# Order of gathers, subtractions and scatters on GpSimd's queue in the expert chunks of a vision-tower kernel

## Chip, cores and metric

The kernel runs on one core of a Trainium2 chip. The metric is the device time of one execution in microseconds (us), as the median of several runs; lower is better.

## What is computed

Thirty-two images of 256 x 256 pass through a wavelet mixing, get a class row in front (257 rows of 256), pass through attention, and then through a mixture of eight experts. Only the last part matters here. Each expert chooses the k rows that score highest for it and adds its result to them:

```python
xf = x.reshape(-1, d)                       # 32 * 257 = 8224 rows, d = 256
k = int(bs * CAPACITY) // n                 # 1028 rows for each of n = 8 experts
vals, idx = jax.lax.top_k(scores.T, k)
kept_w = vals.T
flat_idx = idx.T.reshape(-1)
y = _layernorm(xf[flat_idx].reshape(k, n, d), ln_gamma, ln_beta)
h = jnp.einsum('knd,nfd->knf', y, fc1s) + b1s        # 256 -> 1024
h = jax.nn.gelu(h, approximate=True)
o = jnp.einsum('knf,ndf->knd', h, fc2s) + b2s        # 1024 -> 256
out = xf.at[flat_idx].add((o * kept_w[:, :, None]).reshape(k * n, d))
```

## The kernel before

The program is written engine by engine: each engine has its own instruction list, executed in order, and semaphores tie the lists together. The stage of the experts begins near 340 us and lasts to the end.

**Chunks.** The 1028 rows of an expert are nine tiles (eight of 128 rows, one of 4), and three tiles make a chunk: chunk 0 has tiles 0 to 2, chunk 1 tiles 3 to 5, chunk 2 tiles 6 to 8 (260 columns in all, the "tail"). Here the experts are numbered 0 to 7 in the order in which they are done. `jobs` (L347) walks over the 24 chunks and calls each engine's `emit(prev, cur, nxt, tiles)`: `cur` is the chunk whose first layer is computed, `prev` the one before, whose second layer is computed beside it, `nxt` the one whose rows are turned. A chunk runs in eight slices `f`, one per 128 of the 1024 hidden units.

**Split operands.** Every matmul operand is kept as a high part and a low part (the rest), and three products are summed. So weights and activations are first copied to the high part (`w1h`, `w2h`, `hh`, `yh`), and then the low part is what is left (`w1l`, `w2l`, `hl`, `yl`).

**In a slice** TensorE does six matmuls of the first layer (`first`, L1022) into one of three banks used in turn; ScalarE applies the GELU (L756) and copies the high part (L759); VectorE subtracts for the low part (L1590). TensorE may start slice f only when the low part of slice f-3 is there. Between, TensorE does second-layer matmuls of `prev` (L1036; L1048 for the tail). In slice 3 it turns `nxt`'s gathered rows (`turn`, L1011), which waits for the chunk's gathers.

**Weights.** Both layers of all experts pass through one buffer, `raw`, in two halves. For each half: SyncE loads it (L436) once GpSimd has finished with the half before (`wlo`); ScalarE copies the high part (`high`, L722) in slices 1 and 3; GpSimd subtracts for the low part (`low`, L536), which waits for ScalarE's copy (`whi`). The next expert's first layer (`w1`) is treated in chunk 0 and its second layer (`w2`) in chunk 2. Weight tiles are double: one set for even experts, one for odd.

**Rows in and out.** GpSimd gathers the rows of a tile from DRAM into `yg` (L555) two chunks ahead (`far`), as soon as their indices (`idx`) exist, and scatters each result tile `ob` into the output with an addition (L577), after ScalarE has written it (`weighed`, L772, semaphore `omul`). There are three `ob` buffers; ScalarE writes one again only when its last scatter has landed. In chunks 0 to 2 ScalarE writes the `ob` of chunk c-1 in slices 3, 5 and 7, but those of a tail all in slice 6 of the next chunk 0. `keep_index` (L566, L567) copies an expert's indices for the scatters, in chunk 1.

**Indices.** VectorE makes the indices of an expert two ahead (`place`, L1553 to L1566: `SM`, `rk`, `jk`, `rowf`, `idx`), four tiles of it in chunk 1 and five in chunk 2; with the last tile it prepares the next expert's comparison in two operations over 1028 columns, `ohu` (L1535) and `oh` (L1538). These stand on VectorE ahead of the low part of chunk 2's last slice.

**GpSimd's order.** It is written by hand in `emit` (L589 to L609) and is the same for all chunks of one kind. In chunks 1 and 2 it alternates scatter, gather (and in chunk 2 a subtraction after the second and the third pair); in chunk 0, where the scatters of the tail come last, it is gather, gather, subtraction, gather, subtraction, and then three scatters.

Of the kernel before, what the change touches and what calls it, by code (L numbers as in the profile page):

```python
# [48 lines left out]
def build_program(nc, x, cls_tok, Wa, ba, Wd1, bd1, Wd2, bd2, Wd3, bd3, R, gate_w, gate_wT, gamma, beta,  # L49
                  fc1T, b1, fc2T, b2, b2T, const, out, debug=None):  # L50
    ctx = ExitStack()
    with ctx:
# [206 lines left out]
        def apart(eng):  # L259


            eng.nop(nofuse=True)
# [72 lines left out]
        def flat(weights, half):  # L335

            return weights[:, :, :].rearrange("p a b -> p (a b)")[:, half * NF:(half + 1) * NF]
# [123 lines left out]
        def _(po):  # L461
# [66 lines left out]
            operators(Step(0, 0))  # L528
            po.wait_ge(s["st_set"], 2)
            steps(po, emit, 2)  # L530

            def low(eh, q, layer, half):

                hi, lo = (w1s, w2s)[layer][eh]
                po.wait_ge(s["whi"], (q * 2 + layer) * 2 + half + 1)
                rest = g.tensor_tensor(flat(lo, half), raw[:, half * NF:(half + 1) * NF], flat(hi, half), ALU.subtract)  # L536
                rest.then_inc(s[f"wlo{half}"], 1)
# [12 lines left out]
            def gather(job, t):  # L550

                eh, m = job.eh, SLOTS[t]
                po.wait_ge(s["ixd"], job.q * 9 + t + 1)
                apart(po)
                g.indirect_dma_start(out=yg[eh][0:m, t, :], out_offset=None, in_=rows,  # L555
                                     in_offset=tok(ap=idx[eh][0:m, t:t + 1], axis=0))\
                    .then_inc(s[f"gat{eh}{t // 3}"], 16)

            def keep_index(job):

                eh = job.eh
                if not isinstance(job.q, int) or job.q > 1:
                    for r in range(3):
                        po.wait_ge(s[f"scat{r}"], (job.q - 1) * 48)
                apart(po)
                g.tensor_copy(sidx[eh][:, 0:8], idx[eh][:, 0:8])  # L566
                g.tensor_copy(sidx[eh][0:SLOTS[8], 8:9], idx[eh][0:SLOTS[8], 8:9]).then_inc(s["idc"], 1)  # L567

            def scatter(job, t):
                m = SLOTS[t]  # L570
                po.wait_ge(s["omul"], job.q * 9 + t + 1)
                if t == 0:
                    po.wait_ge(s["idc"], job.q + 1)
                    for r in range(3):
                        after(po, f"scat{r}", job.q * 48)
                apart(po)
                g.indirect_dma_start(out=out_rows, out_offset=tok(ap=sidx[job.eh][0:m, t:t + 1], axis=0),  # L577
                                     in_=ob[t % 3][0:m, :], in_offset=None, compute_op=ALU.add)\
                    .then_inc(s[f"scat{t % 3}"], 16)
# [9 lines left out]
            def emit(prev, cur, nxt, _tiles):  # L589
                split = nxt and cur.q_next and cur.c != 1  # L590

                far = Job(cur.el, cur.k + 2) if cur and (cur.q_next or cur.c == 0) else None
                if far and isinstance(far.q, int) and far.q == 0:
                    far = None

                tail = prev and prev.c == 2
                for u in range(3):
                    if prev and not tail:
                        scatter(prev, prev.t0 + u)
                    if far:  # L600
                        gather(far, far.t0 + u)
                    if split and u:
                        low(1 - cur.eh, cur.q + 1, cur.c // 2, u - 1)
                for u in range(3):
                    if tail:
                        scatter(prev, prev.t0 + u)
                if cur and cur.c == 1 and cur.q_next:
                    keep_index(Job(cur.el, cur.k + 2))
            jobs(po, emit)  # L609


# [1141 lines left out]
```

## Time and profile before

| | |
|---|---|
| median of 3 runs | 786.63 us (785.98 to 787.31) |
| the profiled execution | 786.62 us |
| its span in the trace | 784.8 us |
| TensorE (PE) busy | 696.7 us, 89% |
| VectorE (DVE) busy | 541.0 us, 69% |
| ScalarE (ACT) busy | 459.9 us, 59% |
| GpSimd (POOL) busy | 473.3 us, 60% |

How to read it: times in the trace count from the span's start. An engine is busy while an instruction executes on it; what it waits for in between is given with the engine, the tile and the line that released it. PEld is TensorE's weight load, which lies beside the matmuls, SP is SyncE. An engine that is idle costs nothing by itself; what counts is whether TensorE, or whatever ends last, waited for it. `Lnnn` is a line of the kernel before.

### The profile page before, as it was taken

To read this page: it belongs to the slowest core of one execution; us is meant where nothing else is said; L and a number is where in the kernel's file an instruction comes from. 1 tells how busy PE (TensorE), PEld (TensorE's weight loads), DVE (VectorE), ACT (ScalarE), POOL (GpSimd) and SP (SyncE) were. 2 spreads that over 40 slices of the span, in tenths; PEclk is the share of its full clock that TensorE was granted. 3 is DMA by queue.
4 is the path that set the end of the run, shared out by engine and by line. 5 is a ranking of instruction groups with operands and counts; after the bars stand their busy time and mean duration, and the time that the engine had idled before them with its cause. 6 is when DMAs were issued, how large, how long until landed. Compare 5 with 4: busy or idle time off the path is not lost.

```text
span 784.8 us, 15827 instructions
## 1 busy us (share of the span) xinstructions
PE 696.7 (89%) x4630; PEld 635.5 (81%) x4630; DVE 541.0 (69%) x1885; ACT 459.9 (59%) x1095; POOL 473.3 (60%) x660
## 2 busy tenths in 40 slices
PE   6987999999999945447999999989999999999994
PEld 3986888888888734336989999989889999899993
DVE  3765798998899778987784766756846757634431
ACT  1003588888888869315556656665566566656551
POOL 0258689888988545142366485584674855846523
PEclk9989999999999975559999999999999999999997
DMA  9900022222222228121134243352342432533222
GB/s 258 307 18 1 4 83 81 80 80 81 80 80 81 81 93 170 54 56 61 30 81 117 42 109 89 50 149 43 75 122 41 108 88 42 146 52 49 35 28 27
DMA packets 63563, 64.14 MB, mean 82 GB/s; under 512 B 14032, under 2 KB 57104, under 8 KB 63376
## 3 DMA queue, kind: packets, MB, share of 16 engines
q1 hardware_dynamic: 50576, 46.33, 19.6%
q0 software_dynamic: 12800, 17.12, 13.5%
q8 instruction: 26, 0.43, 0.2%
q14 instruction: 33, 0.27, 0.1%
q10 hardware_dynamic: 128, 0.00, 0.0%
HBM read 37.90 MB, written 25.53 MB: 81 GB/s over the span
## 4 chain that ended last, share of the span: by engine, by line
PE 36%; DVE 7%; issue 6%; ACT 6%; POOL 5%; DMA 3%; POOLq 0%; ACTq 0%; DVEq 0%; SPq 0%
PE bank L1022 16%; PE bank L1036 15%; ACT bank L746 2%; PE bank L1011 2%; PE bank L1048 2%; POOL out L577 2%; POOL w2l L536 1%; POOL yg L555 1%; DMA raw<-in_fc1T 1%; DMA yg<-rows,idx 1%; DVE yl L1583 1%; ACT bank L756 1%; PE bank L1001 1%; DVE jk L1560 1%; ACT hh L759 1%
## 5 line engine op out<-in xcount | busy, mean ns | idle before, releaser
L577 POOL DMA_INDIRECT out<-ob,sidx x72 | 113.9, 1582 | 160.5 <-ACT ob L772 148.8
L1590 DVE TENSOR_TENSOR hl<-bank,hh 128x384 fp32r<-128x384 f32 (+1 forms) x192 | 97.5, 513 | 139.1 <-ACT hh L759 138.6
L756 ACT ACTIVATE bank<-bank,b1s 128x384 f32<-128x384 f32 (+1 forms) x192 | 99.4, 518 | 138.0 <-PE bank L1022 133.5
L1022 PE MATMUL bank<-yh,w1h 128*128 128x384 f32 (+1 forms) x384 | 132.7, 346 | 8.1 <-DVE hl L1590 4.7
L1022 PE MATMUL bank<-yh,w1l 128*128 128x384 f32 (+1 forms) x384 | 123.8, 322 | 0.0
L1022 PE MATMUL bank<-yl,w1h 128*128 128x384 f32 (+1 forms) x384 | 123.3, 321 | 0.0
L1036 PE MATMUL bank<-w2h,hh 128*128 128x256 f32 x384 | 108.1, 281 | 0.0
L1036 PE MATMUL bank<-w2l,hh 128*128 128x256 f32 x384 | 108.0, 281 | 0.0
L1036 PE MATMUL bank<-w2h,hl 128*128 128x256 f32 x384 | 107.9, 281 | 0.0
L555 POOL DMA_INDIRECT yg<-rows,idx x72 | 72.4, 1006 | 44.2 <-issue 39.1
L759 ACT ACTIVATE hh<-bank 128x384 fp32r<-128x384 f32 (+1 forms) x192 | 87.7, 457 | 6.1
L1022 PEld LDWEIGHTS bank<-yh,w1h 128*128 128x128 f32 x384 | 73.8, 192 | 13.0 <-DVE hl L1590 6.0
L1022 PEld LDWEIGHTS bank<-yl,w1h 128*128 128x128 f32 x384 | 73.6, 192 | 0.0
L1022 PEld LDWEIGHTS bank<-yh,w1l 128*128 128x128 f32 x384 | 73.1, 190 | 0.0
L1036 PEld LDWEIGHTS bank<-w2h,hh 128*128 128x128 f32 x384 | 72.7, 189 | 0.0
L1036 PEld LDWEIGHTS bank<-w2l,hh 128*128 128x128 f32 x384 | 72.7, 189 | 0.0
L1036 PEld LDWEIGHTS bank<-w2h,hl 128*128 128x128 f32 x384 | 72.5, 189 | 0.0
L880 PE MATMUL bank<-ET,Rw 128*128 128x256 f32 x256 | 66.1, 380 | 1.7 <-ACT ET L663 1.7
L948 PE MATMUL bank<-GT,ET 128*128 128x137 f32 (+1 forms) x256 | 52.5, 340 | 0.7 <-ACT GT L690 0.7
L504 POOL TENSOR_TENSOR ST<-A,mhalf 128x6 f32<-128x6 f32 x37 | 50.0, 1352 | 3.1
L880 PEld LDWEIGHTS bank<-ET,Rw 128*128 128x128 f32 x256 | 43.8, 191 | 5.6 <-issue 2.1
L290 POOL TENSOR_TENSOR ARENA<-OB,C 128x512 f32<-128x512 f32 x32 | 40.8, 1275 | 12.2 <-ACT OB L637 12.2
(249 smaller groups left out, 1770.6 us busy)
## 6 DMA issues: line engine op xcount, KB each, us to landing
BIG<-in_x SPq DMA_DIRECT2D x4, 2048.0 KB, 16.3
out<-Bs SPq DMA_DIRECT2D x32, 256.0 KB, 2.2
rows<-Yp SPq DMA_DIRECT2D x32, 256.0 KB, 2.4
raw<-in_fc1T SPq DMA_DIRECT2D x16, 512.0 KB
raw<-in_fc2T SPq DMA_DIRECT2D x16, 512.0 KB
yg<-rows,idx POOLq DMA_INDIRECT x72, 2.8
out<-ob,sidx POOLq DMA_INDIRECT x72, 3.8
gwb<-in_gate_w SPq DMA_DIRECT2D x1, 1024.0 KB, 7.2
```

Source lines behind the costliest of these rows:

```text
L290: return ops.tensor_tensor(OP[m.p].rearrange("p g (r k) -> p g r k", k=CG), blocks.unsqueeze(2).to_broadcast(wide), cst("blocks").rearrang ...
L504: g.tensor_tensor(st[:, 8:14], A6[:, :], mhalf[:, :], ALU.pow).then_inc(s["pow"], 1)
L555: g.indirect_dma_start(out=yg[eh][0:m, t, :], out_offset=None, in_=rows, in_offset=tok(ap=idx[eh][0:m, t:t + 1], axis=0))\
L577: g.indirect_dma_start(out=out_rows, out_offset=tok(ap=sidx[job.eh][0:m, t:t + 1], axis=0), in_=ob[t % 3][0:m, :], in_offset=None, compute ...
L746: last = A.activation(sgn[2 * eh + j], V[:, eh, :], ACT.Sign, bias=tried[:, k:k + 1], scale=-1.0, accum_out=cna[eh][:, j:j + 1])
L756: A.activation(h[:, 0:cur.w], h[:, 0:cur.w], ACT.Gelu_apprx_tanh, bias=b1s[:, bass.ds(cur.e, 1), f]).then_inc(s["hact"], 1)
L759: A.activation(hT[cur.p][0][:, f, 0:cur.w], h[:, 0:cur.w], ACT.Copy).then_inc(s["hhi"], 1)
L880: last = T.matmul(Rb[:, e * D:(e + 1) * D], Rw[:, j, e * P:(e + 1) * P], ET[c.p][:, j, 1:NT], start=(j == 0), stop=(j == 1))
L948: T.matmul(Sb[:, c0:c0 + w], ET[c.p][:, j, 1 + h * P:1 + (h + 1) * P], GT[c.p][:, j, 0:w], start=(j == 0), stop=False)
L1022: last = T.matmul(Lb[ring(cur, f)][:, 0:cur.w], w1s[cur.eh][i][:, d, f * P:(f + 1) * P], yT[cur.p][k][:, d, 0:cur.w], start=(n == 0), stop ...
L1036: mm = T.matmul(bank[4 + t % 2][:, 0:D], hT[prev.p][i][:, f, at:at + P], w2s[prev.eh][k][:, f, :], start=(n == 0), stop=(n == 23))
L1590: v.tensor_tensor(hT[cur.p][1][:, f, 0:cur.w], Lb[ring(cur, f)][:, 0:cur.w], hT[cur.p][0][:, f, 0:cur.w], ALU.subtract).then_inc(s["hlo"], 1)
```

## The change

On GpSimd, in each chunk, the three gathers of the far chunk are issued first. Then, for u = 0, 1, 2, the subtraction of half u (in chunks 0 and 2, for u < 2), followed by the scatter u of the previous chunk. The scatters of a tail stay where they were, last in chunk 0. The gather and the scatter themselves, their semaphores and all other engines are as before. Lines from 597 on move by one.

```diff
                 tail = prev and prev.c == 2
+                if far:
+                    for u in range(3):
+                        gather(far, far.t0 + u)
                 for u in range(3):
+                    if split and u < 2:
+                        low(1 - cur.eh, cur.q + 1, cur.c // 2, u)
                     if prev and not tail:
                         scatter(prev, prev.t0 + u)
-                    if far:
-                        gather(far, far.t0 + u)
-                    if split and u:
-                        low(1 - cur.eh, cur.q + 1, cur.c // 2, u - 1)
                 for u in range(3):
                     if tail:
                         scatter(prev, prev.t0 + u)
```

GpSimd's list in chunk 2 of expert 0 (L577 is a scatter of `ob`, L555 a gather into `yg`, L536 a subtraction; the last digit of a name is its buffer), before:

```order
L577 DMA out_0<-ob0,sidx0 8224x256
L555 DMA yg1<-rows,idx1 128x264
L577 DMA out_0<-ob1,sidx0 8224x256
L555 DMA yg1<-rows,idx1 128x264
L536 TENSOR_TENSOR w2l1<-raw,w2h1 128x1024
L577 DMA out_0<-ob2,sidx0 8224x256
L555 DMA yg1<-rows,idx1 128x264
L536 TENSOR_TENSOR w2l1<-raw,w2h1 128x1024
```

and in the change:

```order
L555 DMA yg1<-rows,idx1 128x264 x3
L536 TENSOR_TENSOR w2l1<-raw,w2h1 128x1024
L577 DMA out_0<-ob0,sidx0 8224x256
L536 TENSOR_TENSOR w2l1<-raw,w2h1 128x1024
L577 DMA out_0<-ob1,sidx0 8224x256
L577 DMA out_0<-ob2,sidx0 8224x256
```

The three gathers have moved to the head, the first subtraction from behind the second scatter to ahead of the first, and the second from behind the third scatter to behind the first.

The next place on GpSimd is chunk 0 of expert 1, with the tail's scatters at its end, before:

```order
L555 DMA yg1<-rows,idx1 128x264 x2
L536 TENSOR_TENSOR w1l0<-raw,w1h0 128x1024
L555 DMA yg1<-rows,idx1 4x264
L536 TENSOR_TENSOR w1l0<-raw,w1h0 128x1024
L577 DMA out_0<-ob0,sidx0 8224x256
```

and in the change:

```order
L555 DMA yg1<-rows,idx1 128x264 x2
L555 DMA yg1<-rows,idx1 4x264
L536 TENSOR_TENSOR w1l0<-raw,w1h0 128x1024 x2
L577 DMA out_0<-ob0,sidx0 8224x256
```

Here only the third gather and the first subtraction have changed places.

## Rows read from the trace of the kernel before

**Rows 1.** Page: busy time of each engine.

```profile
PE 696.7 (89%) x4630; PEld 635.5 (81%) x4630; DVE 541.0 (69%) x1885; ACT 459.9 (59%) x1095; POOL 473.3 (60%) x660
```

**Rows 2.** By stretch: length, busy us (count) of PE, PEld, DVE, ACT, POOL, clock, DMA.

```profile
526.96:545.55 18.59, 18.59 (x130) 18.09 (x131) 10.88 (x35) 9.98 (x22) 8.94 (x7) 1.00 0.33 64
545.55:561.82 16.27, 15.87 (x132) 15.38 (x132) 12.31 (x45) 10.66 (x23) 8.19 (x9) 1.00 0.31 51
...
717.76:734.07 16.31, 15.81 (x111) 15.24 (x109) 6.84 (x15) 9.71 (x21) 12.14 (x9) 1.00 0.29 55
```

**Rows 3.** The same view: chunk 0 of experts 1 to 6.

```profile
404.26:421.80 17.54, 16.10 (x111) 15.20 (x109) 11.18 (x22) 11.49 (x23) 15.79 (x10) 1.00 0.48 137
...
561.82:580.09 18.27, 16.10 (x111) 15.21 (x109) 11.54 (x21) 11.45 (x23) 15.98 (x10) 1.00 0.49 133
...
sum 107.12, PE 96.83 PEld 91.25 DVE 68.39 ACT 69.03 POOL 95.69; mean PE 16.14 PEld 15.21 DVE 11.40 ACT 11.51 POOL 15.95
```

**Rows 4.** Line L722 from 340 us: its engine's idle time (us, times), by releaser.

```profile
  DMA raw<-in_fc1T: 24.1, 12
```

**Rows 5.** ScalarE in order of time: start, us, instruction, idle before.

```profile
496.46 1.05 ACT L722 ACTIVATE w2h<-raw 128x1024 fp32r<-128x1024 f32 x1
...
500.63 1.05 ACT L722 ACTIVATE w2h<-raw 128x1024 fp32r<-128x1024 f32 x1
...
515.86 1.06 ACT L722 ACTIVATE w1h<-raw 128x1024 fp32r<-128x1024 f32 x1 [2.44 <-DMA raw<-in_fc1T]
...
521.55 1.06 ACT L722 ACTIVATE w1h<-raw 128x1024 fp32r<-128x1024 f32 x1 [2.51 <-DMA raw<-in_fc1T]
```

**Rows 6.** Chain of waits, in order of time: start, us, what.

```profile
515.17 2.42 POOL w2l L536
...
517.74 3.79 DMA raw<-in_fc1T
...
526.96 1.15 PE bank L1022 x5
```

**Rows 7.** GpSimd in order of time, expert 2's end and expert 3's chunk 0.

```profile
495.21 1.57 POOL L577 DMA_INDIRECT out<-ob,sidx  x1 [1.71 <-ACT ob L772]
...
502.85 1.60 POOL L577 DMA_INDIRECT out<-ob,sidx  x1 [4.42 <-ACT ob L772]
...
506.48 1.57 POOL L577 DMA_INDIRECT out<-ob,sidx  x1 [0.71 <-ACT ob L772]
...
509.40 2.41 POOL L536 TENSOR_TENSOR w2l<-raw,w2h 128x1024 fp32r<-128x1024 f32 x1
511.98 1.85 POOL L577 DMA_INDIRECT out<-ob,sidx  x1 [0.17 <-issue]
...
527.46 1.63 POOL L577 DMA_INDIRECT out<-ob,sidx  x1 [1.55 <-ACT ob L772]
```

**Rows 8.** VectorE in order of time: ohu of expert 0, then around 510.

```profile
350.84 0.73 DVE L1535 TENSOR_SCALAR ohu<-iot,begM 128x1028 bf16<-128x1028 f32 x1
...
509.84 2.54 DVE L1535 TENSOR_SCALAR ohu<-iot,begM 128x1028 bf16<-128x1028 f32 x1
...
513.72 1.35 DVE L1590 TENSOR_TENSOR hl<-bank,hh 128x260 fp32r<-128x260 f32 x3
```

**Rows 9.** TensorE in order of time, at the start of slice 2.

```profile
514.19 0.44 PE L1022 MATMUL bank<-yh,w1h 128*128 128x384 f32 x1 [0.85 <-DVE hl L1590]
```

**Rows 10.** GpSimd in order of time, expert 0.

```profile
350.45 1.25 POOL L555 DMA_INDIRECT yg<-rows,idx  x1 [1.28 <-DVE idx L1566]
...
354.91 2.38 POOL L536 TENSOR_TENSOR w1l<-raw,w1h 128x1024 fp32r<-128x1024 f32 x1 [0.89 <-ACT w1h L722]
```

**Rows 11.** GpSimd in order of time, chunk 1 of expert 3.

```profile
537.89 1.59 POOL L577 DMA_INDIRECT out<-ob,sidx  x1 [5.28 <-ACT ob L772]
```

**Rows 12.** TensorE in order of time, turning rows in expert 7.

```profile
727.44 0.85 PE L1011 MATMUL bank<-C,yg 128*128 128x128 f32 x6 [0.50 <-DMA yg<-rows,idx]
```

**Rows 13.** VectorE in order of time, expert 0.

```profile
356.48 0.27 DVE L1556 TENSOR_SCALAR rk<-C,SM 128x1 f32<-128x1 f32 x1
```

## Prediction

> **What bounds the kernel now.** I read the views from wide to narrow. The page first: TensorE is busy 89% of the span [rows 1], and in the experts' stage its granted clock is full [rows 2, 3], so the stage of the experts, which is all that the diff touches, is bound by TensorE unless something starves it. Then the busy time by stretch, one stretch per chunk, cut where TensorE starts the first matmul of the chunk. Chunk 1 of expert 3 lasts 18.59 us and TensorE is busy for all of it; chunk 2 lasts 16.27 with 15.87 busy [rows 2]. Chunk 0 is another matter: in experts 1 to 6 it lasts 17.54 to 18.27 us, 107.12 in all, with 96.83 busy [rows 3]. Expert 7's chunk 0 has the same matmuls (x111 against x110 or x111) and lasts 16.31 [rows 2]. So there are about 2 us per expert to be had, in chunk 0 and hardly anywhere else.
>
> Who starves it: ScalarE's copy of the next expert's first-layer weights (L722, w1h<-raw) found its engine idle for 24.1 us over 12 times, until the transfer into raw had landed [rows 4]. Twelve is two halves times six experts. The two waits of expert 3 are 2.44 and 2.51 us [rows 5]; everything behind them on ScalarE, the activations of TensorE's products, is late with them. The chain of waits says where this comes from: GpSimd's subtraction w2l (515.17), the transfer into raw (517.74), and then, through ScalarE's copy w1h and the activations behind it, TensorE's next chunk (526.96) [rows 6]. raw is one buffer for both layers, so the first-layer weights are fetched only when GpSimd has subtracted the second-layer ones. GpSimd's own rows show why it subtracts late: both inputs, w2h, were ready in the middle of chunk 2 (copies at 496.46 and 500.63) [rows 5], but the subtractions ran at 509.40 and 515.17 [rows 6, 7], because each stood behind scatters that waited for ScalarE's results (4.42 and 0.71 us idle), and behind gathers queued after those scatters [rows 7].
>
> A second stall stands in the same place. VectorE's ohu takes 0.73 us at 350.84 and 2.54 us at 509.84 [rows 8]. In the second case it ran under GpSimd's subtraction (509.40 to 511.81) and ended 0.57 us after it. VectorE's hl for the last slice of chunk 2 queues behind ohu and oh, starts at 513.72, and TensorE stood 0.85 us for it [rows 8, 9]. So I put the 1.8 us of difference down to GpSimd's subtraction, not to ohu's own work. The Trainium skill (SBUF — State Buffer, SBUF: two separate sides) says that GpSimd and a two-port VectorE operation take a shared port pair as an exclusive lock, the loser blocking fully; by that rule the trace agrees.
>
> **The change, part by part.** No instruction is added or removed; all of it is order on GpSimd.
>
> Chunk 2, the part that matters. GpSimd ends chunk 1's last scatter at 496.78 (495.21 + 1.57) and its index copies 0.3 later. Now come three gathers at 1.0 us and a gap of 0.3 each, until 501.0; their indices were made an expert earlier. The first subtraction needs 2.4 us [rows 7] and w2h's first half, ready at 497.5: it runs 501.0 to 503.4, not 509.40 to 511.81. The first scatter follows (its ob was ready at 502.8, so it is 0.8 late), 1.85 us, then the second subtraction, about 505.6 to 508.1, not 515.17 to 517.59. The two other scatters start near 508.3 (was 506.48) and 510.3 (was 511.98).
>
> - Transfers. ScalarE's copy began 4.05 us after the first subtraction's end (511.81) and 3.96 after the second's (517.59), load and all [rows 5, 6, 7]. With the same lags the halves land at 507.5 and 512.1. ScalarE wants them at 513.42 (515.86 less its 2.44 of waiting) and at 516.6 (521.55 less both waits). Slack 5.9 and 4.5 us: both waits go, even if a transfer took twice as long beside the gathers and scatters.
> - ohu at 509.84 now meets no subtraction, which ended 1.7 us before; a scatter is under way instead. At 350.84 it met a gather (350.45 to 351.70) and took 0.73 [rows 8, 10]. I take 0.73, so VectorE is 1.8 us earlier and TensorE's 0.85 go.
> - The late scatters cost nothing: ob is written again in chunk 0's sixth slice, whose first scatter was at 527.46 [rows 7], over 15 us on.
>
> Chunk 0: gathers, both subtractions, then the tail's scatters. The subtractions wait for w1h, now at about 514.5 and 519, and end near 518.5 and 521.4, ahead of the tail's scatters; their results are wanted an expert later. Costed at nothing.
>
> Chunk 1: three gathers before the first scatter, 4.0 us. The cover is GpSimd's idle 5.28 us there before the scatter at 537.89 [rows 11]. Were it gone, a scatter would be late by the rest, with its buffer free for many us more: still nothing. TensorE is full in chunk 1, so nothing is gained either.
>
> What chunk 0 then lasts: the row nearest is expert 7's, which has no weight copies, no ohu, and the same matmuls: 16.31, of which 0.50 is TensorE waiting for a gather [rows 2, 12]: that of tile 5, which GpSimd's order put behind the last scatter of the chunk before, and which now goes out at that chunk's head. So 15.8. The two copies, 2.1 us of ScalarE, come on top of expert 7's 9.71 busy, 11.8 in 15.8: they fit, and I add nothing for them.
>
> **Sum.** Experts 1 to 6: 6 x 15.8 = 94.8 against 107.12, 12.3 less. Expert 7: 0.5 less. Expert 0: GpSimd's order in chunk 0 is the same, nothing. Together 12.8, so the profiled execution's 786.62 us becomes **773.8**; the median of the runs, 786.63, is the same time. Bounds: below, TensorE's busy time alone in the six chunks gives no more than 107.12 - 96.83 = 10.3, but that busy time includes stretched matmuls (16.1 against 15.8 in expert 7); with 15.6 per chunk and the 0.4 us idle of chunk 2 also gone in seven experts the gain would be 16. Above, half the waits left, see the rivals.
>
> **Rivals.**
> 1. *Only the transfer's waits go.* If gathers take longer and the second subtraction slips by the 1.7 us of margin, it falls on ohu again. TensorE keeps its 0.85 us six times: 773.8 + 5.1 = 778.9. For it: the margin is small and was computed through six GpSimd steps. Against: every step's row repeats within 0.1 us from expert to expert.
> 2. *One of the two transfer waits stays*, or ScalarE, with two copies inside a shorter chunk, becomes the limit of its last four slices. About half of the 2 us per expert comes back: 773.8 + 6 = 780. Against: the slacks of 5.9 and 4.5 us.
> 3. *Slower: the subtractions now hold up VectorE in chunk 2.* There VectorE makes indices (rk, rowf, idx) from SBUF, and TensorE already idles 0.4 us [rows 2]. If each of 14 moved subtractions held one of its operations as long as ohu was held, 1.8 us, that is 25.2 us; less 12.8, the kernel would take 799. It decides from 0.9 us each. Against: rk at 356.48 ran inside a subtraction (354.91 to 357.29) and took 0.27 [rows 10, 13], its usual. The skill's page puts under the lock also operations with two SBUF inputs against a GpSimd that reads SBUF; in chunk 2 only oh is one, and it stands behind ohu.
> 4. *No change.* ScalarE's waits were in the shadow of something else, and chunk 0 keeps its length, 786. Against: expert 7's is shorter by 1.2 us or more.
>
> **How the numbers follow.** Forecast 0.73, rival 1 0.12, rival 2 0.07, rival 3 0.04, rival 4 0.04. The forecast's own range is 771.3 (gain 15.3, chunk 0 near 15.6 and part of chunk 2's idle) to 776.5 (0.5 us per expert less than hoped). The range for 8 in 10 goes on to 779.3, which takes in rival 1 and part of rival 2. A measurement can tell 0.2%, 1.6 us: forecast and rivals 1 and 2 are faster, 0.92; rival 4 is the same, 0.04; rival 3 slower, 0.04.
>
> **What would show it.** Right: no idle time of L722 on raw<-in_fc1T; w2l subtractions that end before ohu begins; all ohu near 0.73 us; chunk 0 near 15.8 us in experts 1 to 6, chunk 1 still 18.6. Wrong: ohu at 2.5 (rival 1); L722 waits of over 0.5 us (rival 2); chunk 2 longer than 16.3 with VectorE named as TensorE's releaser (rival 3); a chunk 0 of 17.5 with some other releaser in ScalarE's place (rival 4).

## Result and the profile after

The changed kernel takes **775.31 us** (median of 4 runs, 774.18 to 777.41) against 786.66 us (785.98 to 787.31) for the kernel before in the same set of runs: a ratio of 0.9859 with a 95% interval of 0.9843 to 0.9874, some 11.3 us less. In a later set of runs it took 773.26 us against 785.69, ratio 0.9847 (0.9833 to 0.986); one execution of the kernel before in that set was slow, 1752.38 us, and stands outside the ratio. The profiled execution of the first set is its longest, 777.41 us, with a span of 775.6.

First the page: GpSimd (POOL) is busy for about as long as before, VectorE (DVE) 10.5 us less [rows 1], since its comparisons are no longer stretched.

```profile
PE 696.2 (90%) x4630; PEld 636.8 (82%) x4630; DVE 530.5 (68%) x1885; ACT 460.9 (59%) x1095; POOL 476.5 (61%) x660
```

Chunk 0 of experts 1 to 6 in the view by stretch (length, then busy us and count of PE, PEld, DVE, ACT, POOL, clock, DMA):

```profile
405.89:421.52 15.63, 15.63 (x111) 15.23 (x109) 9.64 (x22) 11.63 (x23) 9.98 (x6) 1.00 0.45 116
...
506.86:522.65 15.79, 15.64 (x110) 15.24 (x109) 9.77 (x21) 11.69 (x23) 10.72 (x7) 1.00 0.50 122
...
sum 94.52, PE 93.89 PEld 91.48 DVE 58.35 ACT 69.55 POOL 63.20; mean PE 15.65 PEld 15.25 DVE 9.72 ACT 11.59 POOL 10.53
```

94.52 us stand where 107.12 stood [rows 3], and TensorE is busy for 93.89 of them. The same view for chunk 1 and 2 of expert 3 (they answer to [rows 2]), and chunk 0 of expert 7:

```profile
522.65:541.23 18.58, 18.58 (x130) 18.08 (x131) 10.88 (x35) 10.06 (x22) 10.77 (x8) 1.00 0.33 62
541.23:557.71 16.48, 16.10 (x133) 15.45 (x132) 12.12 (x45) 10.56 (x23) 12.20 (x10) 1.00 0.40 83
709.51:725.16 15.65, 15.65 (x111) 15.25 (x109) 6.85 (x15) 9.73 (x21) 6.03 (x5) 1.00 0.23 36
```

Chunk 1 is unchanged. Chunk 2 is 0.21 us longer, and in experts 4 and 5 it is 17.16 and 17.18 us where it was 15.99 and 16.27: the change gave something back there (experiment 5). GpSimd in order of time, around the start of expert 3's chunk 0 at 506.86, where [rows 7] had the subtractions at 509.40 and 515.17 for a chunk that began at 508.70:

```profile
497.54 0.95 POOL L555 DMA_INDIRECT yg<-rows,idx  x1 [0.30 <-issue]
498.52 2.40 POOL L536 TENSOR_TENSOR w2l<-raw,w2h 128x1024 fp32r<-128x1024 f32 x1
501.62 1.62 POOL L577 DMA_INDIRECT out<-ob,sidx  x1 [0.70 <-issue]
502.70 2.98 POOL L536 TENSOR_TENSOR w2l<-raw,w2h 128x1024 fp32r<-128x1024 f32 x1
505.85 1.59 POOL L577 DMA_INDIRECT out<-ob,sidx  x1 [0.17 <-issue]
509.17 2.46 POOL L577 DMA_INDIRECT out<-ob,sidx  x1 [1.72 <-ACT ob L773]
```

The second subtraction now ends at 505.68, before the chunk begins. (Its record overlaps that of the scatter before it, so its start is rough.) VectorE and ScalarE in order of time, for [rows 8] and [rows 5]:

```profile
508.00 0.76 DVE L1536 TENSOR_SCALAR ohu<-iot,begM 128x1028 bf16<-128x1028 f32 x1
508.89 1.29 DVE L1539 SCALAR_TENSOR_TENSOR oh<-iot,finM,ohu 128x1028 bf16<-128x1028 f32 x1
```

```profile
511.48 1.05 ACT L723 ACTIVATE w1h<-raw 128x1024 fp32r<-128x1024 f32 x1
...
515.99 1.05 ACT L723 ACTIVATE w1h<-raw 128x1024 fp32r<-128x1024 f32 x1
```

ohu takes 0.76 instead of 2.54 us, and ScalarE's two weight copies stand without a bracket: no idle time before them. The view of that line (L723 now) has no entry under its idle time, where [rows 4] had 24.1 us:

```profile
its engine sat idle before it (us, times) until:
who waited for it (us, times):
  POOL w1l L536: 2.6, 2
```

### The profile page after: what moved, and what is told of

The parts are those of the page before. It is cut to its first block, busy times and chain, and to the rows that moved or that the text cites. A ratio compares the mean times of both kernels' runs of the same rounds, so it can differ in the third digit from the quotient of the medians.

```text
span 775.6 us, 15827 instructions
## 1 busy us (share of the span) xinstructions
PE 696.2 (90%) x4630; PEld 636.8 (82%) x4630; DVE 530.5 (68%) x1885; ACT 460.9 (59%) x1095; POOL 476.5 (61%) x660
## 4 chain that ended last, share of the span: by engine, by line
PE 44%; DVE 8%; ACT 6%; issue 2%; POOL 1%; another core or an unknown queue 1%; DMA 0%; POOLq 0%; ACTq 0%; DVEq 0%
PE bank L1023 21%; PE bank L1037 14%; PE bank L1049 5%; ACT bank L747 2%; PE bank L1012 2%; DVE yl L1584 2%; DVE jk L1561 1%; ACT bank L757 1%; PE bank L1002 1%; ACT hh L760 1%; ACT jk L747 1%; DVE rk L1557 1%; DVE hl L1591 1%; DVE bank L1576 0%
## 5 line engine op out<-in xcount | busy, mean ns | idle before, releaser
L577 POOL DMA_INDIRECT out<-ob,sidx x72 | 118.1, 1640 | 147.2 <-ACT ob L773 122.5
L555 POOL DMA_INDIRECT yg<-rows,idx x72 | 71.9, 998 | 45.0 <-issue 40.2
```

## Where chunk 0's time went, slice by slice

These sums over experts 1 to 6 are worked out from the starts of TensorE's first matmul of each slice. "The change" is its second profile, where chunk 2 gave back least. The last column is chunk 2 of experts 2 to 5 together.

| kernel | chunk 0 | its slice 1 | slice 6 | slice 7 | chunk 2, experts 2 to 5 |
|---|---|---|---|---|---|
| before | 107.12 | 19.22 | 14.07 | 10.15 | 64.53 |
| the change | 94.45 | 13.51 | 9.69 | 8.42 | 65.42 (first profile 67.24) |
| chunks 0 and 1 alone | 107.10 | 19.10 | 14.46 | 10.13 | 64.55 |
| chunk 2 alone | 94.44 | 13.53 | 9.70 | 8.44 | 64.55 |
| second half last | 97.12 | 13.51 | 11.08 | 9.69 | 65.51 |
| before, ohu not held | 110.02 | 14.11 | 21.24 | 10.35 | 64.71 |
| the change, VectorE later | 102.13 | 20.47 | 9.73 | 8.41 | 64.53 |

Of the 12.7 us, 5.7 come from slice 1 (VectorE behind ohu) and 6.1 from slices 6 and 7 (ScalarE behind the second transfer). The last rows of the table are kernels of the experiments below.

## Experiments

Each kernel was timed against the kernel before on its chip. Line numbers in its rows are its own.

**1. The new order in chunk 2 alone.** NEW and OLD stand for the loops of the diff.

```diff
+                if cur and cur.c == 2:
+                    NEW
+                else:
+                    OLD
```

> GpSimd's new order in chunk 2 alone; in chunks 0 and 1 the order of before. My theory (all of the gain comes from the second-layer subtractions being done 8 to 9 us earlier in chunk 2, which ends ScalarE's waits for raw and the collision with ohu): 775.3 us, within 1.6 us of the change, chunk 0 of experts 1 to 6 near 15.7 us, ohu 0.73 us. Rival (the gathers and subtractions of chunk 0, or the gathers of chunk 1, carry half of it): 780 us or more.

Measured: 773.09 us (771.18 to 773.69), ratio 0.9825 (0.9799 to 0.9852). The whole gain is in chunk 2's order.

**2. The new order in chunks 0 and 1 alone.** The condition is `cur.c != 2`.

> The new order in chunks 0 and 1 alone; in chunk 2 the order of before. My theory: 786.6 us, within 1.6 us of before, ScalarE's waits for raw<-in_fc1T still about 24 us in 12 times, ohu 2.5 us. Rival (half of the gain lies here): 781 us.

Measured: 785.93 us (783.95 to 787.61), ratio 0.9994 (0.9981 to 1.0008): nothing. ohu is held again, and the view of ScalarE's weight copy shows the waits:

```profile
  DMA raw<-in_fc1T: 23.2, 12
```

**3. The change, with VectorE made about 2 us later ahead of ohu.** Three more comparisons into scratch tiles; the transfers stay early.

```diff
+                if not isinstance(job.q, int) or job.q > 1:
+                    for n, spare in enumerate((ge, eq, sc)):
+                        v.tensor_scalar(spare[:, :, :].rearrange("p a b -> p (a b)"), iot[:, 0:2 * NT], 0.0, None,
+                                        ALU.is_ge, ALU.add, accum_out=(need[:, 0:1], need[:, 1:2], mm2[:, 0:1])[n])
```

> The change, with three operations of no use on VectorE (514 columns each, some 2.0 us together) ahead of ohu for the last six experts: the delay that the collision made, without a collision. In the trace of the change the low part hl of chunk 2's last slice is done at 510.6 and TensorE wants it at 511.3. If VectorE's delay has a price of its own, 2.0 us less 0.7 of slack is 1.3 us six times: 783 us. Rival (ScalarE's waits were the whole loss and the 0.85 us of TensorE for hl would have been made up later): 775.3 us, within 1.6 us.

Measured: 781.18 us (780.87 to 783.1), ratio 0.9938 (0.9918 to 0.9958). By the ratios that is 6.2 or 7.2 us more than the change (0.9859 or 0.9847), and in the traces chunk 0 of the six experts is 7.7 us longer. TensorE's waits from 400 to 730 us name VectorE's hl in experts 1 to 6 (engine line, releaser, us, times, longest):

```profile
PE bank L1023 <- DVE hl L1595: 6.0, 6, 1.0
```

Slice 1 is back at 3.35 to 3.46 us (3.01 to 3.28 before, 2.25 in the change), slices 6 and 7 are not. VectorE's hl starts 5.21 us after the start of chunk 0 (513.29 less 508.08), 5.02 in the kernel before and 3.24 in the change, so the delay made here is 0.2 us larger than the one it stands for. A VectorE that is late by 1.8 to 2.0 us then costs TensorE about 1 us per expert, also where no transfer is late: the stretched ohu was a cost by itself, worth about half of the gain.

**4. The kernel before, with an ohu that is not held.** The comparison gets an accumulated output, which makes it another form of instruction.

```diff
-                v.tensor_scalar(ohu[:, c0:c1], iot[:, c0:c1], begM[:, bass.ds(job.el, 1), job.eh], None, ALU.is_ge)\
+                v.tensor_scalar(ohu[:, c0:c1], iot[:, c0:c1], begM[:, bass.ds(job.el, 1), job.eh], None, ALU.is_ge,
+                                ALU.add, accum_out=junk1[:, :])\
                     .then_inc(s[begun], 1)
```

> The kernel before, with ohu written as a comparison that also accumulates its sum (a form that I take not to collide with GpSimd's subtraction, and to last 1.1 to 1.3 us instead of 2.5). GpSimd's order is that of before, so ScalarE still waits for raw. My theory: TensorE's 0.85 us in front of slice 2 goes, but the end of chunk 0 is set by the second transfer's landing, so nothing is gained: 786.6 us, within 1.6 us. Rival (the two stalls add up, each with its own price): 786.6 - 6 x 0.85 = 781.5 us. If ohu still takes 2.5 us, the run says nothing on this.

Measured: 792.46 us (791.3 to 792.98), ratio 1.0079 (1.0056 to 1.0102), **slower** than before, where neither theory had it. VectorE, then GpSimd, in order of time, expert 3:

```profile
511.62 1.28 DVE L1536 TENSOR_SCALAR_CACHE_REDUCE ohu<-iot,begM 128x1028 bf16<-128x1028 f32 x1
512.83 0.08 DVE L1536 DVE_READ_ACCUMULATOR ohu<-iot,begM 128x1 f32 x1
513.04 1.62 DVE L1540 SCALAR_TENSOR_TENSOR oh<-iot,finM,ohu 128x1028 bf16<-128x1028 f32 x1
```

```profile
511.16 2.41 POOL L537 TENSOR_TENSOR w2l<-raw,w2h 128x1024 fp32r<-128x1024 f32 x1
513.74 2.39 POOL L578 DMA_INDIRECT out<-ob,sidx  x1 [0.17 <-issue]
516.43 1.00 POOL L556 DMA_INDIRECT yg<-rows,idx  x1 [0.30 <-issue]
517.46 2.41 POOL L537 TENSOR_TENSOR w2l<-raw,w2h 128x1024 fp32r<-128x1024 f32 x1
```

ohu runs inside the subtraction at 1.28 us, and slice 1 falls by 5.1 us over six experts. oh, which begins 0.53 us before that subtraction ends, takes 1.62 us, not 1.29. And the scatter now starts 0.70 us after oh did, where in the kernel before it started 0.53 us ahead of oh, under the end of ohu; it takes 2.39 us instead of 1.85 [rows 7]. So the second subtraction behind it comes later in the chunk (7.00 us after its start, 6.47 before), and with it the second transfer. ScalarE waits 3.36 us for it, not 2.51 [rows 5], in all 29.6 us over 12 times:

```profile
523.80 1.06 ACT L723 ACTIVATE w1h<-raw 128x1024 fp32r<-128x1024 f32 x1 [3.36 <-DMA raw<-in_fc1T]
```

Slice 6 grows by 7.2 us over six experts. In the kernel before, then, the two delays overlap: taking one away hands its time to the other, with interest. Of the 4.7 us by which the profiled execution (791.30) is longer than that of the kernel before, chunk 0 of these six experts has 2.9; 1.0 lies in expert 0's first two chunks, which differ by as much between the other kernels here, and 0.7 in one chunk 1. Of the kernels run here, those that move the subtractions out of the way are the ones that remove both delays.

**5. The change again.** No edit.

> The changed kernel once more, unaltered. In its first profile ScalarE began the fourth GELU of chunk 2 in experts 2 to 5 1.1 to 1.9 us after TensorE's product was done, and chunk 2 of these experts lasted 16.42 to 17.18 instead of 15.98; the kernel with the new order in chunk 2 alone was 2.2 us faster and showed none of it. Theory 'sporadic': that lateness belongs to the execution; the median stays near 775.3 but this profile shows another pattern, perhaps none, and a profiled execution without it is near 774.7 (777.4 less 2.7). Theory 'order': it belongs to the order of the requests in chunks 0 and 1; then the same four rows are here again, with chunk 2 near 16.4 to 17.2.

Measured: 773.26 us (772.74 to 774.12), ratio 0.9847 (0.9833 to 0.986). The same four rows are late, by 1.02 to 1.06 us now. The first profile, expert 4's chunk 2 in order of time (GpSimd, ScalarE, VectorE; releasers are inferred, so "remote" names no one); TensorE's product was done at 599.16:

```profile
599.21 0.95 POOL L555 DMA_INDIRECT yg<-rows,idx  x1 [0.30 <-issue]
...
600.18 2.41 POOL L536 TENSOR_TENSOR w2l<-raw,w2h 128x1024 fp32r<-128x1024 f32 x1
...
601.01 0.45 ACT L757 ACTIVATE bank<-bank,b1s 128x260 f32<-128x260 f32 x1 [2.89 <-remote]
...
601.91 0.43 DVE L1591 TENSOR_TENSOR hl<-bank,hh 128x260 fp32r<-128x260 f32 x1 [1.76 <-ACT hh L760]
```

The second profile, same place, product done at 596.21:

```profile
596.26 0.96 POOL L555 DMA_INDIRECT yg<-rows,idx  x1 [0.30 <-issue]
...
597.26 0.45 ACT L757 ACTIVATE bank<-bank,b1s 128x260 f32<-128x260 f32 x1 [2.09 <-PE bank L1023]
```

So the place is the kernel's, as the theory 'order' had it, and its size varies: 1.1 to 1.9 us late and 2.7 us more in chunk 2 in the one, 1.0 to 1.1 late and 0.9 more in the other. Usually ScalarE starts 0.10 to 0.12 us after the product. That the orders of chunks 0 and 1 are what matters is not shown by this run.

The lateness reaches TensorE through VectorE: hl, then the layer norm of the turned rows, then the index operation jk queue behind the GELU. TensorE's waits in the first profile, from 400 to 730 us, have (0.3 us, once, in the kernel before):

```profile
PE bank L1002 <- DVE jk L1561: 3.3, 8, 0.8
```

Two things more are in the traces. Experts 2 to 5 are those of the loop in `jobs`; expert 1 is written out ahead of it, has the same gather 0.01 to 0.03 us after the same product in the two profiles, and its GELU is on time (0.10 us). And in neither profile do the DMA queues that load instructions carry a packet from 592 to 606 us, so no loading of instructions is seen at expert 4's late GELU.

**6 and 7. The new order in chunks 0 and 2, and in chunks 1 and 2.** Conditions as in experiment 1, with `cur.c != 1` and `cur.c != 0` for the new order.

> The new order in chunks 0 and 2, the old one in chunk 1. Chunk 0 of experts 1 to 6 stays at 15.6 to 15.9. If the three gathers ahead of the scatters in chunk 1 are what the change loses against the kernel that has the new order in chunk 2 alone (773.1), this one is at 773.1 and chunk 2 lasts 15.98; if chunk 0's order is, it is at 775.3; if neither is and the lateness of ScalarE is sporadic, anything from 773 to 775.3.

> The new order in chunks 1 and 2, the old one in chunk 0 (where it delays the two w1l subtractions until after two gathers). Mirror of the run with chunks 0 and 2: if chunk 0's order is the loss, 773.1; if chunk 1's is, 775.3 with chunk 2 of some experts over 16.4 us. If these two kernels and the change agree within 1 us, neither part is the loss.

Measured: chunks 0 and 2, 776.38 us (774.93 to 776.77), ratio 0.9879 (0.9864 to 0.9895); chunks 1 and 2, 774.08 (772.35 to 774.65), ratio 0.9846 (0.9831 to 0.9861). Neither is simply the loss. The second repeats the change's late GELU (chunk 2 of experts 2 to 5 65.50 us in all). The first loses at another place: in chunk 2 of experts 0 and 2 to 5, VectorE begins the work on the turned rows 1.25 to 1.34 us after TensorE's transposes are done (0.49 in expert 1; 0.03 to 0.04 in the kernel before), and chunk 2 of experts 2 to 5 takes 66.53 us, 2.0 more than in experiment 1; here in expert 4, where they were done at 601.33 (600.51 + 0.82):

```profile
602.63 1.27 DVE L1585 TENSOR_SCALAR bank<-bank,gam,bet 128x384 f32<-128x384 f32 x2 [1.61 <-PE bank L1021]
```

The kernel of experiment 1 has GpSimd's gathers at the same distance from the start of chunk 2 (5.9 us both) and starts that instruction at once (598.97, transposes done 598.93). I had no place for this in either expectation.

**8. The second subtraction behind all three scatters of chunk 2.**

```diff
                 for u in range(3):
-                    if split and u < 2:
+                    if split and (u == 0 or u == 1 and cur.c == 0):
                         low(1 - cur.eh, cur.q + 1, cur.c // 2, u)
                     if prev and not tail:
                         scatter(prev, prev.t0 + u)
+                if split and cur.c == 2:
+                    low(1 - cur.eh, cur.q + 1, 1, 1)
```

> The change, but the second subtraction of w2l goes behind all three scatters of chunk 2, the first stays ahead of them. By the changed kernel's rows the third scatter ends at 511.6 in expert 3, so the subtraction runs from there to 514.0 and its transfer lands near 518.0 (lag 3.96), where ScalarE wants it at chunk start 506.9 + 7.9 = 514.8: the first wait of L723 gone (6 of 12 left), the second near 3.2 us. If chunk 0 pays for the wait of the second half alone, its length goes to 16.5 to 17.5 and the kernel to 775.3 + 6 x 1.2 = 782, between 779.5 and 785.5. Rival: ScalarE has slack behind the second copy, TensorE does not notice, chunk 0 stays under 16.0 and the kernel under 777. ohu should stay at 0.73, since the subtraction begins after it.

Measured: 776.46 us (775.92 to 779.1), ratio 0.9896 (0.9878 to 0.9915): nearer to the rival, though chunk 0 does go over 16.0 us, in experts 3 to 6 (16.06 to 16.58). Chunk 2 has the change's late GELU here too (65.51 us in experts 2 to 5). Six waits are left:

```profile
  DMA raw<-in_fc1T: 9.6, 6
```

```profile
515.81 1.06 ACT L725 ACTIVATE w1h<-raw 128x1024 fp32r<-128x1024 f32 x1 [1.90 <-DMA raw<-in_fc1T]
```

The transfer lands as forecast, 11.13 us after the chunk's start (515.81 less 504.68). What was off is when ScalarE wants it: 9.2 us after the start, not 7.9. I had taken 7.9 from the kernel before by striking out both waits; but with both gone ScalarE waits for TensorE's product of slice 3, and that sets the time. Six waits, 9.6 us, cost TensorE 2.7 us in chunk 0 (97.12 less 94.45). It is not a fixed share of each: the waits are 1.30, 1.16, 1.90, 1.94, 1.42 and 1.83 us in experts 1 to 6, and their chunks 0 are 0.17, 0.02, 0.75, 0.77, 0.27 and 0.69 us longer than in the change's second profile. So the first 1.15 us of such a wait are slack, and what goes beyond costs TensorE its full length.

**9. Chunk 2 spread out: subtraction, scatter, gather, and so on.**

```diff
+                if cur and cur.c == 2:
+                    for u in range(3):
+                        if split and u < 2:
+                            low(1 - cur.eh, cur.q + 1, 1, u)
+                        if prev:
+                            scatter(prev, prev.t0 + u)
+                        if far:
+                            gather(far, far.t0 + u)
+                else:
+                    NEW
```

> A candidate for a better order of chunk 2, chunks 0 and 1 as in the change: subtraction, scatter, gather, subtraction, scatter, gather, scatter, gather. Both subtractions still end before ohu and both transfers are in time, so chunk 0 of experts 1 to 6 at 15.6 to 15.9 and no idle time of ScalarE's copies. If the late fourth GELU of chunk 2 (TensorE's product done 0.05 us before the third gather begins, GELU 1.05 us late) hangs on three gathers in a row, it is gone, chunk 2 of experts 2 to 5 lasts 15.98 to 16.3 and the kernel is 0.5 to 1.5 us faster than the change on the same chip (ratio to before near 0.983). If the two orders are worth the same, 0.9835 to 0.986.

Measured: 773.97 us (772.49 to 774.27), ratio 0.9846 (0.9833 to 0.986). The late GELU is gone (chunk 2 of experts 2 to 5 64.52), but expert 7's chunk 0 is at 16.24 us with 0.44 idle for a gather again, as in [rows 12], since a gather stands last in chunk 2, and no difference to the change can be measured.

**10. Chunk 2 with the first subtraction ahead of the gathers.**

```diff
+                if cur and cur.c == 2 and split:
+                    low(1 - cur.eh, cur.q + 1, 1, 0)
                 if far:
...
-                    if split and u < 2:
+                    if split and (cur.c == 0 and u < 2 or cur.c == 2 and u == 1):
```

> Chunk 2: the first subtraction ahead of the three gathers, the second between the scatters as in the change. The first half then is there 4 us earlier, of which ScalarE needs nothing: no gain from that. The gathers come 2.4 us later, their rows are wanted an expert later: no loss. Rival: a gather that moves lets a waiting engine be late somewhere else, as the run with chunks 0 and 2 had VectorE 1.3 us late in chunk 2; then some slice of chunk 2 is 0.3 to 1.2 us longer in all experts and the ratio is 0.987 or more, not 0.9835 to 0.986.

Measured: 772.76 us (771.31 to 773.21), ratio 0.9839 (0.9826 to 0.9853). No late GELU, chunk 2 at 64.52, and no new lateness.

**11. The change with its gathers in chunk 2 a little later.** A memset of a scratch tile at the head of chunk 2.

```diff
+                if cur and cur.c == 2:
+                    g.memset(idle[:, :], 0.0)
```

> The change with a small GpSimd memset (256 B per partition, some 0.1 to 0.3 us) at the head of chunk 2, which shifts gathers and subtractions by that much. Theory 'coincidence': ScalarE's fourth GELU of chunk 2 is late because its semaphore comes as the third gather begins; shifted, the lateness of 1.05 us in experts 2 to 5 is gone or has moved to another instruction. Theory 'none of the gathers' doing' (the kernel with VectorE's three extra operations had the same coincidence, 0.04 us, and no late GELU): the same four rows are late by 1.0 to 1.9 us whatever the shift. Chunk 0 stays at 15.6 to 15.9 either way.

Measured: 772.25 us (771.3 to 772.76), ratio 0.9828 (0.9813 to 0.9843). The third gather of expert 4's chunk 2 now starts 0.15 us after the product is done (596.53) instead of 0.05, and ScalarE starts in its usual time:

```profile
596.68 0.95 POOL L556 DMA_INDIRECT yg<-rows,idx  x1 [0.30 <-issue]
...
596.64 0.45 ACT L760 ACTIVATE bank<-bank,b1s 128x260 f32<-128x260 f32 x1 [1.16 <-PE bank L1026]
```

That chunk in the view by stretch, of this kernel and then of the change's second profile:

```profile
589.48:605.47 15.99, 15.87 (x132) 15.37 (x132) 12.31 (x45) 10.66 (x23) 12.34 (x11) 1.00 0.40 84
```

```profile
589.16:605.52 16.36, 16.07 (x132) 15.42 (x132) 12.12 (x45) 10.46 (x23) 12.19 (x10) 1.00 0.40 82
```

An extra instruction on GpSimd gives 0.37 us back in this chunk and 0.90 in the four. Theory 'none of the gathers' doing' falls: a shift of 0.1 us removes all four. But the coincidence alone is not the cause either. In experiment 3 the product was done 0.04 us before the third gather too, and the GELU was on time (third gather at 602.96, GELU at 603.02, idle 1.16), and so it is in expert 1 of the change itself (experiment 5). What else must meet there, and what held ScalarE, stays open; experiment 6 shows that VectorE can be held in a like way.

## Why the prediction was right

- **Chunk 0.** 15.8 us each, 94.8 in all, for experts 1 to 6; measured 15.63 to 15.85, 94.52. Expert 7 to be 0.5 shorter; it is 15.65 instead of 16.31, 0.66. The two stretches that the prediction put in the sum are exact to 0.5 us.
- **The subtractions.** Counted from the start of chunk 0, the first was to begin 7.7 us ahead (501.0 to 508.70) and begins 8.3 ahead (498.52 to 506.86); the second was to end 0.6 ahead and ends 1.2 ahead. So the margin to ohu, forecast as 1.7 us, is 2.3, and rival 1 did not happen. Some 0.4 us of each surplus is no merit of the order: chunk 2 of expert 2 itself ends 0.42 us late (16.42 us instead of 16.00). Rival 1's price, 5.1 us, is somewhat under what the runs show: 5.7 us in slice 1 between before and after, and 6.2 to 7.2 us in experiment 3, whose VectorE is 0.2 us later still.
- **The transfers.** Both waits are gone, as forecast. By the forecast's own lags from subtraction to copy, slack of the first 5.9 forecast, 6.5 found (498.52 + 2.40 + 4.05 against 511.48); of the second 4.5 forecast, 6.4 found (505.68 + 3.96 against 515.99): experiment 8 shows why. Rival 2 priced one wait that stays at 6 us; the six waits that experiment 8 left cost 2.7 in chunk 0.
- **ohu.** 0.73 us forecast, 0.73 to 0.76 found. It was put down to GpSimd's subtraction and not to its own work; in experiment 2 the subtraction stands over it again and ohu takes 2.53. The forecast's reason for 0.73, that a scatter beside ohu would not stretch it, is not tested by experts 1 to 6 of the change, where ohu meets none; under a scatter it takes 0.73 to 0.83 us in experiment 1 and 0.86 to 0.98 in experiment 3. By the Trainium skill (SBUF — State Buffer, SBUF: two separate sides) GpSimd and a two-port VectorE operation take a shared port pair as an exclusive lock; the trace agrees for ohu, if it is such an operation. For oh, which reads two tensors from SBUF, the page has the lock only against a GpSimd operation that reads SBUF. Here a scatter that starts under oh ends 1.45 us after it (509.17 + 2.46 against 508.89 + 1.29) and takes about 1.6 us alone, as if it had begun when oh ended. That fits the page's rule if the scatter counts as an operation that reads SBUF, which no run here tells. Experiment 4 shows the same: 513.74 + 2.39 is 1.47 after oh's end.
- **Chunks 0 and 1.** Costed at nothing; experiment 2 measured 0.9994. Right for the two beside the old chunk 2. With chunk 2's new order they are not free, since they decide what meets what there (experiments 5 to 7).
- **Chunk 2 was the step that failed.** The prediction left it at its old length, and rival 3 looked for VectorE's index operations being held by the subtractions. These are not: rk and jk keep 0.27 and 0.49 us. Yet the sign that the prediction set for rival 3 is there, a chunk 2 over 16.3 us with VectorE as TensorE's releaser: jk, 3.3 us in 8 times, 2.7 of them in experts 2 to 5 (experiment 5). So the sign did not tell the rival apart. Behind it stands ScalarE's late GELU, 2.7 us in the profiled execution and 0.9 in the second profile; its cause stays open. The rest of the difference in the first profile lies before chunk 0 of expert 1: the stage begins 0.54 us later, and expert 0's first two chunks take 40.11 instead of 39.04 us. The first of the two ran at a granted clock of 0.76 (0.86 before), the second at 0.94 (0.95). In the change's second profile the two take 38.39, and in the thirteen profiles 38.02 to 40.11, so I don't put this down to the order; it also means that kernels 1 us apart may differ there alone. Together: 12.60 + 0.66 - 2.71 - 1.07 - 0.54 = 8.9, against the 9.2 by which 777.41 is under 786.62. That the median came within 1.5 us of the forecast is in part luck: chunk 0 and expert 7 gained 0.5 us more than the sum had, and chunk 2 gave back what the sum did not have.

The forecast of 12.8 us is thus the gain of chunk 0 and expert 7 without what chunk 2 gives back; the kernels without the late GELU and with expert 7's gain (experiments 1, 10 and 11) measure it, by their ratios, as 13.8, 12.7 and 13.5 us, each to about 1 us, the first to 2. (The upper end of the forecast's own range, 776.5, is 0.3 us under the reason given for it, six times 0.5 us on top of 773.8; the measured median lies under both.)

## What to carry to other kernels

Where one engine's queue feeds a transfer that another engine will wait for, put the operation that frees the buffer ahead of work that waits for late results: here the order of one engine's queue in one chunk of three was worth 1.7% by itself (experiment 1). Two delays that overlap must be priced together: taking ohu alone out of its collision made the kernel 0.8% slower, and the trace shows what stood behind it, oh, in the next one. A wait that is left over costs nothing up to its slack (1.15 us in experiment 8) and all of the rest, so a mean share of it misleads. And once the large waits are gone, profiles of neighbouring orders, even of one with a useless 0.1 us shift, should be compared chunk by chunk: a late start without a visible cause can be worth 1 to 3 us.

## What the runs showed of the hardware

- ohu as a plain comparison takes 0.73 to 0.76 us alone, 0.73 to 0.98 where it starts under a scatter (experiments 1 and 3), and 2.35 to 2.54 under a GpSimd subtraction; with an accumulated output it takes 1.26 to 1.28 us, under the subtraction as well as alone.
- A scatter on GpSimd takes 1.6 us alone and 2.3 to 2.6 when it starts 0.2 to 0.8 us after oh does, ending 1.4 to 1.5 us after oh. When it started 0.5 us ahead of oh, under the end of ohu [rows 7, 8], it took 1.85 and oh 1.29: the two orders are not alike.
- An engine whose semaphore should be there can start 1.0 to 1.9 us late at a fixed place of the program, on ScalarE (a GELU of experts 2 to 5) or VectorE (1.25 to 1.34 us, in experts 0 and 2 to 5), and a shift of GpSimd's queue by 0.1 us removed ScalarE's. At the loop's turn (expert 4, chunk 0, slice 0) ScalarE's first GELU starts 2.6 to 3.8 us after its product in all thirteen profiles, of the kernel before too.
